# A fused recurrent-attention layer: from steps of 128 tokens of one sequence to steps of 256 tokens of two sequences, with several values kept features-on-partitions

## The reference

```
xn = layernorm(x)
q, k, v = silu(xn @ Wq), silu(xn @ Wk), silu(xn @ Wv)          # [4,512,16,16]
# per head, with decay exp(ld): S_t = exp(ld) S_{t-1} + k_t v_t^T ; o_t = q_t S_t
gate = (xn @ Wg1) @ Wg2                                        # rank 16
o = o * sigmoid(gate); o = o * rsqrt(mean over a head of o*o + 1e-5); o = o * norm_w
s = o @ Wo
g = silu( dequant(fp8(xn * scale)) @ dequant(fp8(W2 * scale1)) )
out = x + s * g
```

## Time and profile before

| | us |
|---|---|
| three runs, median (lowest, highest) | 189.59 (189.05, 189.99) |
| the profiled execution: device time | 189.03 |
| its span, first to last instruction | 187.1 |
| PE busy / DVE busy / POOL busy / ACT busy | 166.7 / 147.3 / 104.6 / 103.1 |
| mean granted TensorE clock, share of full speed | 0.958 |

### The profile page before, as it was taken

One profiled execution on the slowest core, in us unless ns is written; L12 is line 12 of the kernel. 1 busy time (PEld: TensorE's weight loads), 2 busy tenths in 40 slices (PEclk: granted clock), 3 DMA queues, 4 the chain that ended last, 5 costly groups with the idle time before them and its releaser, 6 DMA issues.

```text
span 187.1 us, 7410 instructions
## 1 busy us (share of the span) xinstructions
PE 166.7 (89%) x2510; PEld 127.1 (68%) x2510; DVE 147.3 (79%) x548; ACT 103.1 (55%) x283; POOL 104.6 (56%) x180
## 2 busy tenths in 40 slices
PE   4868469999999999999999999999999999998392
PEld 4745248677777777777777777777777777776181
DVE  1789985979797979888888879797979697857672
ACT  3584446483839383847575665748483847372100
POOL 6654871747565666656574656575747474732210
PEclk9999966999999999999999999999999999999657
DMA  5295300000100010000000000000000000010000
GB/s 145 71 254 166 112 5 0 4 4 4 33 0 32 0 33 4 30 4 28 0 28 0 28 0 27 1 0 28 0 28 0 28 0 28 0 33 4 28 28 28
DMA packets 7201, 5.82 MB, mean 31 GB/s; under 512 B 1744, under 2 KB 7184, under 8 KB 7184
## 3 DMA queue, kind: packets, MB, share of 16 engines
q1 hardware_dynamic: 7184, 5.60, 9.9%
HBM read 3.50 MB, written 2.10 MB: 30 GB/s over the span
## 4 chain that ended last, share of the span: by engine, by line
PE 61%; DVE 12%; ACT 11%; issue 8%; POOL 3%; DMA 3%; SPq 1%; ACTq 0%; DVEq 0%; POOLq 0%
PE b_scores L1081 11%; PE b_xo L1180 8%; PE b_att L1107 5%; PE b_kv L1028 4%; PE b_kv L1033 3%; PE b_kv L1030 3%; PE b_qg L1028 3%; ACT qT L526 3%; PE b_scores L1124 3%; PE b_gate L1067 3%; ACT ffn_silu L509 2%; DVE og L747 2%; ACT e_y L561 2%; PE b_att L1143 2%; PE b_qg L1033 2%
## 5 line engine op out<-in xcount | busy, mean ns | idle before, releaser
L1081 PE MATMUL b_scores<-qT,kT 32*64 32x128 f32 x512 | 31.6, 283 | 1.5 <-DVE probs L717 1.2
L717 DVE TENSOR_TENSOR probs<-b_scores,decay_mask 128x256 f32<-128x256 f32 x64 | 26.6, 418 | 2.6 <-PE b_scores L1081 2.3
L1081 PEld LDWEIGHTS b_scores<-qT,kT 32*64 32x64 f32 x512 | 20.1, 132 | 12.2 <-issue 8.9
L545 ACT ACTIVATE xn<-x_sb,shift,rstd 128x256 f32 (+1 forms) x15 | 9.0, 602 | 35.1 <-DVE shift L681 35.1
L375 POOL TENSOR_TENSOR state_c<-state,own_head 128x256 f32<-128x256 f32 x28 | 20.7, 738 | 11.3 <-DVE state L733 10.2
L345 POOL TENSOR_TENSOR e_sum<-e_y,e_magic 128x256 f32<-128x256 f32 x16 | 11.7, 729 | 25.0 <-DVE e_magic L692 25.0
L384 POOL TENSOR_TENSOR on<-og,og_rs 128x256 f32<-128x256 f32 x15 | 9.3, 622 | 17.3 <-DVE og_rs L776 15.5
L774 DVE SCALAR_TENSOR_TENSOR og_half<-og_y,og_var 128x16 f32<-128x16 f32 x48 | 14.7, 306 | 0.7
L392 POOL TENSOR_TENSOR y<-sg,x_sb 128x256 f32<-128x256 f32 x15 | 11.0, 731 | 6.1 <-DVE sg L787 6.1
L772 DVE TENSOR_TENSOR og_y<-og_rs 128x16 f32<-128x16 f32 x48 | 13.7, 285 | 0.8
L1124 PE MATMUL b_scores<-probs,v_parity 64*32 64x64 f32 x1024 | 14.0, 229 | 0.2 <-DVE probs L717 0.2
(11 more groups left out here) (135 smaller groups left out, 458.7 us busy)
## 6 DMA issues: line engine op xcount, KB each, us to landing
out_dram<-y SPq DMA_DIRECT2D x16, 128.0 KB, 1.7
x_sb<-in_L_attn_x_dram SPq DMA_DIRECT2D x3, 512.0 KB, 3.5
x_sb<-in_L_attn_x_dram SPq DMA_DIRECT2D x1, 384.0 KB, 5.4
w_f<-in_L_attn_Wk_dram SPq DMA_DIRECT2D x1, 256.0 KB, 2.9
w_f<-in_L_attn_Wv_dram SPq DMA_DIRECT2D x1, 256.0 KB, 3.1
w_f<-in_L_attn_Wq_dram SPq DMA_DIRECT2D x1, 256.0 KB, 3.4
w_f<-in_L_ffn_input_dram SPq DMA_DIRECT2D x1, 256.0 KB, 4.1
wo_f<-in_L_attn_Wo_dram SPq DMA_DIRECT2D x1, 256.0 KB, 3.9
```

The source lines that it names most:

```text
L717: v.tensor_tensor(probs[:, r], b_score[r % 2][:, 0:4 * C].rearrange("p (i c) -> p i c", i=4), decay_mask[:, r], ALU.mult).then_inc(s_probs, 1)
L1081: mm = t.matmul(b_score[r % 2][c * C:c * C + C, half * 2 * C:(half + 1) * 2 * C], kT[rows, u, half, c * C:c * C + C], qT[rows, u, half, :, ...
```

## The change

The kernel is written anew. A step now holds 128 tokens of each of two sequences (`S` = 2, `T` = 256 tokens), so there are 8 steps in place of 16; sequence pairs alternate (`pair(n) = n % 2`). The loop is unrolled, with one program line per instruction. These things change in what is done:

- q comes out of its projection with features on partitions (`project_q`), and the Silu for each head parity is taken straight from PSUM, so q is not transposed. The gate's rank-16 values, the gate, the attention output, the FP8 input and the norm stand features-on-partitions too, so the transposes of the gate's stack, of the quantised x and of the output go.
- The state is kept as 32x32 blocks (`state_steps`, `from_state`), and `from_chunk` adds straight into the output in PSUM; `add_chunk` and its copy go.
- The sums over heads are products with a matrix of halves (`head_sums`), and the reciprocal root works on 128x64 in 11 instructions. GpSimd spreads it (`spread_rs`) and TensorE broadcasts it to the features by two float32 products; VectorE then does the head norm.
- The output projection is float32 in one part, in place of three fp32r parts.
- The decayed q goes from VectorE to GpSimd; the last add of the FP8 rounding goes from GpSimd to VectorE.
- All products of `keep_warm` go, as does one Newton-seed instruction.

```diff
-                    t.matmul(dst, xT_hi[:, kk], w_hi[:, kk, a:b], start=(kk == 0), stop=False)
-                for kk in range(KH):
-                    t.matmul(dst, xT_hi[:, kk], w_lo[:, kk, a:b], start=False, stop=False)
-                pe.wait_ge(s_xTlo, num(i, j) + 1)
-                for kk in range(KH):
-                    mm = t.matmul(dst, xT_lo[:, kk], w_hi[:, kk, a:b], start=False, stop=(kk == KH - 1))
-                mm.then_inc(s_done, 1)
...
+            def project_q(n):
+                u = n % 2
+                pe.wait_ge(s_xThi, n + 1)
+                need(pe, s_sg, n - 2)
+                for part in (w_hi, w_lo):
+                    for half in range(KH):
+                        for kk in range(KH):
+                            t.matmul(ps_q[:, half], part[:, 0, kk, half * P:half * P + P], xT_hi[:, u, kk],
+                                     start=(part is w_hi and half == 0 and kk == 0), stop=False, skip_group_check=True)
+                pe.wait_ge(s_xTlo, n + 1)
+                for half in range(KH):
+                    for kk in range(KH):
+                        mm = t.matmul(ps_q[:, half], w_hi[:, 0, kk, half * P:half * P + P], xT_lo[:, u, kk],
+                                      start=False, stop=(kk == KH - 1), skip_group_check=True)
+                for s in range(S):
+                    tok = slice(s * P, s * P + P)
+                    for kk in range(KH):
+                        t.matmul(dst[:, s], xT_hi[:, u, kk, tok], w_hi[:, w, kk], start=(s == 0 and kk == 0), stop=False, skip_group_check=True)
+                        t.matmul(dst[:, s], xT_hi[:, u, kk, tok], w_lo[:, w, kk], start=False, stop=False, skip_group_check=True)
+                    for kk in range(KH):
+                        mm = t.matmul(dst[:, s], xT_lo[:, u, kk, tok], w_hi[:, w, kk], start=False, stop=(kk == KH - 1), skip_group_check=True)
...
-                    t.transpose(ps_qT[:, kk, :], q[:, kk * P:kk * P + P], ident[:])
-                        mm = t.matmul(ps_state[b * C:b * C + C, half, :], kd[rows, u, cols],
-                                      kv[rows, u, D + cols.start:D + cols.stop], start=True, stop=True)
-                                mm = t.matmul(ps_avT[32 * r:32 * r + 32, half, c, :],
-                                              v_parity[rows, u, par * D + half * P + 32 * r:par * D + half * P + 32 * r + 32],
-                        t.matmul(ps_o[c * C:c * C + C, half * P:half * P + P], qdT[:, u, half, c * C:c * C + C],
-                                 st[:, half, :], start=(half == 0), stop=False, skip_group_check=True)
-                        mm = t.matmul(ps_o[:, half * P:half * P + P], avT[:, half, :], ident[:],
-                                      start=False, stop=True, skip_group_check=True)
-                    mm = t.transpose(ps_oT[:, kk, :], on[:, kk * P:kk * P + P], ident[:])
-                parts = [(oT_hi, wo_hi), (oT_hi, wo_lo), (oT_lo, wo_hi)]
-                for n, (lhs, rhs) in enumerate(parts):
-                    for kk in range(KH):
-                        mm = t.matmul(ps_out, lhs[:, kk], rhs[:, kk], start=(n == 0 and kk == 0), stop=(n == 2 and kk == KH - 1))
...
+                for half in range(KH):
+                    mm = t.matmul(ps_gate[:, half], wg2_stack[:, half * P:half * P + P], g1T[:], start=(half == 0), stop=True, skip_group_check=True)
+                else:
+                    pe.wait_ge(s_probs, 4 * n + r - 1)
+                            mm = t.matmul(ps_score[r % 2][c * C:c * C + C, cols], kT[rows, u, half, tok],
+                                          q_par[rows, u, :, half, tok], start=True, stop=True, skip_group_check=True)
+                mm.then_inc(s_score, 1)
+                                mm = t.matmul(ps_u[32 * r:32 * r + 32, c, half, s], kd[rows, u, s, half * P + 32 * r:half * P + 32 * r + 32],
+                                              heads[:, s * HH + half * 4 + r, :, 0:E], start=True, stop=True, skip_group_check=True)
+                mm.then_inc(s_u, 1)
+                pe.wait_ge(s_qd, n + 1)
+                pe.wait_ge(s_ownmid, n + 1)
+                if pos(n) < NB - 1:
+                    pe.wait_ge(s_end, ends(n))
+                if pos(n) > 0:
+                    pe.wait_ge(s_ownend, ends(n - PAIRS))
+                                t.matmul(ps_o[rows, c, z:z + C], st, qd[rows, u, half, s * P + c * C:s * P + c * C + C],
+                                         start=(half == 0 and s == 0), stop=False, skip_group_check=True)
+                                    mm = t.matmul(ps_o[32 * r:32 * r + 32, c, z:z + C], v_par[rows, u, blk:blk + 2 * E],
+                                                  probs[rows, r, s, i:i + C],
+                                                  start=(c == 0 and pos(n) == 0 and half == 0 and s == 0 and par == 0),
+                                                  stop=(par == 1), skip_group_check=True)
+                mm.then_inc(s_ops, 1)
+            def head_sums(n):
+                pe.wait_ge(s_sq, n + 1)
+                            mm = t.matmul(ps_sum[32 * j:32 * j + 32], head_sum[:, half, 0:32], og_sq[:, c, z:z + C],
+                                          start=(half == 0), stop=(half == KH - 1), skip_group_check=True)
+            def spread_rs(n):
+                pe.wait_ge(s_spread, n + 1)
+                if known(n + 2):
+                    pe.wait_ge(s_xTlo, n + 3)
+                for half in range(KH):
+                    mm = t.matmul(ps_rs[:, half], head_spread[:, half], rs_spread[:].rearrange("p j t -> p (j t)"),
+                                  start=(half == 0), stop=True, skip_group_check=True)
+                mm.then_inc(s_rsps, 1)
+            def project_o(n):
+                pe.wait_ge(s_on, n + 1)
+                if known(n + 2):
+                        mm = t.matmul(ps_out[:, s], on[:, kk, s * P:s * P + P], wo_scaled[:, kk], start=(s == 0 and kk == 0),
+                                      stop=(kk == KH - 1), skip_group_check=True)
+                mm.then_inc(s_outps, 1)
...
+                nxt, cur, back = known(n + 1), known(n), known(n - 1)
+                if n == -1:
+                    pe.wait_ge(s_wlo, 1)
+                if cur:
+                    scores(n, 0)
+                    scores(n, 1)
+                if nxt:
+                if cur:
+                    scores(n, 2)
+                    scores(n, 3)
+                if nxt:
+                    project_k(n + 1)
+                if cur:
+                    state_steps(n)
+                if nxt:
+                    project_g1(n + 1)
+                if back:
+                    spread_rs(n - 1)
+                if nxt:
+                    project_v(n + 1)
+                    if n == -1:
+                    if n == -1:
+                    ffn(n + 1)
+                if cur:
+                    from_state(n)
+                    from_chunk(n)
+                if known(n + 2):
+                    transpose_x(n + 2)
+                if nxt:
+                    transpose_k(n + 1)
+                if back:
+                    project_o(n - 1)
+                if cur:
+                    head_sums(n)
...
+                g.tensor_tensor(e4_sum[:], e4_y[:], e4_magic[:], ALU.add).then_inc(s_e4sum, 1)
+                pool.wait_ge(s_e4sum, n + 1)
+                need(pool, s_xqT, n)
+                g.tensor_tensor(e4_q[:], e4_sum[:], e4_magic[:], ALU.subtract).then_inc(s_e4q, 1)
+                g.tensor_tensor(rs_spread[:], og_rs[:].unsqueeze(1).broadcast_to([P, 4, C]),
+                                own_block[:].unsqueeze(2).broadcast_to([P, 4, C]), ALU.mult).then_inc(s_spread, 1)
+                g.tensor_tensor(y[:, n % 2], sg[:].rearrange("p (s d) -> p s d", s=S), x_sb[:, x_tiles(n), :], ALU.add).then_inc(s_y, 1)
...
+                nxt, cur, back = known(n + 1), known(n), known(n - 1)
+                if nxt:
+                    round_y(n + 1)
+                if nxt:
+                    decay_q(n + 1)
+                if back:
+                    spread_rs(n - 1)
+                if nxt:
+                    decay_k(n + 1)
+                if cur:
+                    own_state_mid(n)
+                    own_state_end(n)
+                if known(n - 2):
+                    add_x(n - 2)
+                if known(n + 3):
+                    norm_factors(n + 3)
...
+                if known(n + 2):
+                    high_xT(n + 2)
+                    scale_y(n + 2)
+                if nxt:
+                    copy_kT(n + 1)
+                if cur:
+                    square_o(n)
...
+                v.tensor_tensor(probs[:, r], ps_score[r % 2].rearrange("p (s z) -> p s z", s=S),
+                                decay_mask[:, r].unsqueeze(1).broadcast_to([P, S, 4 * C]), ALU.mult).then_inc(s_probs, 1)
+                v.scalar_tensor_tensor(out=og[:], in0=gate_tanh[:, n % 2], scalar=1.0, in1=ps_o,
```

(45 more changed lines are left out.)

1499 lines of the change are left out of this document (614 added, 885 removed).

## The result

The changed kernel takes 199.09 us (median of 4 runs, 197.87 to 202.58), the kernel before 189.42 beside it: ratio 1.0487, 95% interval 1.0427 to 1.0546, slower by 4.9%. The forecast was 187.0. The profiled execution took 197.87, its span (first to last instruction) 196.1, against 184.5 forecast for the span: 11.6 us to find.

The account below looks back on a forecast made before the run. TensorE was taken to bound the kernel: 15.3 us of work plus 3.5 of waits per cycle, 18.8 with switches. With both ends the span came to 184.5, plus 1.9 outside and 0.56 for the median: 187.0 us, range 171 to 196.

Parts of the forecast that it names:

- F0: End of step 0's from_chunk products, which frees TensorE (F in any cycle): forecast at 44.7 us.
- undisturbed period, 18.8: TensorE's cycle for 256 tokens: 15.3 us of work and 3.5 of waits, 18.8 with half of the rounded-away switches.
- hindrance of VectorE by GpSimd: VectorE instructions with two SBUF inputs, and find_nan, wait out GpSimd's: TensorE waits 1.4 us at mask 0, 1.0 before FFN.
- slower rival: GpSimd's decayed q stops VectorE's root once more, delaying mask 0: period 20.0, 194 us in all; 24%.
- step 1 17.3: Step 1, without output add and with half of the state products, was to take 17.3 us.
- handover to the head sums: After the output projection TensorE waits for ScalarE's square before the head sums: stall 0.35 us.
- this rival: TensorE's clock stays low over many cycles; dismissed as having little for it, with no chance of its own.
- From the chunk: 1.55: TensorE's products from the chunk: 32 took 0.79 us, so 64 of the same shape take 1.55 per cycle.
- the number of records is what is equal: Reason for costing the 32 smaller state products at 0.8 us, between bounds of 0.38 and 0.79.
- the 15.3 of the sum: TensorE's work in a new cycle, all products added: 15.3 us against 19.44 before.

Follow-up runs that it names:

- a_addx: Changed kernel with GpSimd's add of the output moved from behind the masked end state to behind spread_rs: 197.63 us, or 195.41 without disturbed runs.
- a_warm: Changed kernel plus 56 idle identity products (before the first FFN, first scores, first head sums, and in the drain): 194.46 us, ratio 1.0296.
- a_combo_inter: Changed kernel with idle products, moved output add, masks 0 and 1 before the whole root, and two score groups taken product by product: 184.16 us, ratio 0.9746.
- a_combo: Changed kernel with 56 idle products, moved output add, and masks 0 and 1 ahead of the whole reciprocal root: 185.36 us, ratio 0.9734.
- ci_split: a_combo_inter with the row of 128 chunk products cut in half by the transposes of x and k: 183.62 us, ratio 0.9711.
- b_twice_loop: Kernel before, loop kept, with each chunk's products of probabilities and values computed twice: 219.67 us, or 217.8 without disturbed runs.
- a_split: Changed kernel with the row of 128 chunk products cut in half by the transposes of x and k: 205.81 us, ratio 1.0878.

## Why the prediction was wrong

**Right.** The rows of single parts: F0 at 44.98 (44.7 forecast), the first scores at 32.08 (31.2), the row of 128 records 1.41 to 1.49 (1.55), the state products 0.69 (0.8, with bounds of 0.38 and 0.79), the output projection 1.89 (1.8), the broadcast 1.03 (0.9), the next scores 3.29 behind F (3.4). The undisturbed period, 18.8, to the tenth, twice. And the hindrance of VectorE by GpSimd, the cause of both waits in the cycle (0.92 each, where 1.4 and 1.0 were forecast):

```profile
113.32 1.29 POOL L324 TENSOR_TENSOR e_q<-e_sum,e_magic 128x512 bf16<-128x512 f32 x1
113.33 1.36 DVE L647 TENSOR_TENSOR og_y<-og_rs 128x64 f32<-128x64 f32 x1
...
122.32 1.29 POOL L363 TENSOR_TENSOR y<-sg,x_sb 128x512 f32<-128x512 f32 x1
122.40 1.36 DVE L585 TENSOR_SCALAR e_nan<-e_q 128x512 bf16<-128x512 bf16 x1
```

og_y takes 1.36 us under GpSimd's rounding, 0.23 alone, and find_nan 1.36 under the output's add, 0.29 alone (a_addx). The hindrance of the slower rival, by the decayed q, came too (og_y at 116.32, 0.71 us), behind mask 0 and so at no price: the slower rival's mechanism did not decide. The Trainium skill (SBUF — State Buffer, "Who interferes with whom") holds here as it did in the prediction: VectorE waits out the whole instruction that was first.

**Wrong, two terms that stood at nothing.**
1. *Step 1's clock.* The step that failed is "step 1 17.3", with the low clock put only on step 0's first 3 us and on the end of the drain. I had costed the handover to the head sums at 0.35, from a steady cycle. In step 0 there is no output projection beside it, so TensorE idles 1.93 us at 47.99, after a step 0 that itself had holes, and the clock is 0.50 from 50 to 62 us. Price in us: 22.9 - 17.3 - 0.9 for the stop in it = 4.7; a_warm, with its products there, does the step in the 17.3 of the forecast. I had let this rival go with "the waits are 1.5 and 1.0 us in a cycle", without looking at the one step that differs.
2. *Stops without a wait.* "From the chunk: 1.55" took 0.79 for 64 records and doubled it. The time of a record was right (128 in 1.41), but in four of the rows TensorE also stops for 0.9 to 1.5 us, and once behind one: 0.89 + 0.94 + 1.41 + 0.93 + 1.52 = 5.7. A row of 64 in the kernel before shows no such stop in 16, nor in 16 written out; rows of 128 do, in that kernel too. The kernel before could not show it, but the same step had written "the number of records is what is equal" and never asked how many records a microsecond TensorE can be given over a longer stretch; the new cycle has 192 in 2.5 us, where the old had 64 amid wide ones.

Together 10.4 of the 11.6 us. The other 1.2 are the drain, 27.9 us against 26.7, and that is the clock again: the last step's states and chunk, forecast to end 9.5 us behind its first scores, end 10.75 behind them (168.18 to 178.93), and what follows takes 17.2 as forecast. The forecast had the low clock from the broadcast on only.

```profile
172.00:178.00 6.00, 6.00 (x210) 4.62 (x211) 2.62 (x7) 0.00 (x0) 2.24 (x3) 0.50 0.15 49
```

That the sum closes to the tenth is in part luck: against the forecast, F0 is 0.3 late, steps 2 and 3 are 0.6 longer than their stops explain and step 6 is 1.0 shorter.

A smaller term was wrong too and hidden: a pair of score groups takes 1.52, not 1.05, because groups written one behind the other overlap less than I read from 4 products in a group to 8 in two; a_combo_inter shows 1.03 with the right order. In the changed kernel the first pair's excess lies in the wait for mask 0 (0.92 waited where 1.45 was forecast), and for the second the forecast had masks as the bound anyhow, 1.65 for both groups. So the work of a cycle is not the 15.3 of the sum: with both waits gone, a_combo still takes 16.9, and TensorE is busy for 16.5 of 16.8 us in it (63.7 to 80.5).

That the stops are the fetching of instructions is the reading that fits all of it: fixed places in the program whatever the times, evenly spaced in its records, a shift by inserted instructions, none at 64 records, many at 128, and the same 1.2 to 1.6 us from the end of a packet to TensorE's next product. Fewer stops when wide products part the same instructions fit too, but weakly (ci_split). What stays open is how early a packet is asked for, and why the third turn of the loop in b_twice_loop has to fetch where the kernel before does not.

## What to carry to other kernels

Count instructions, not only columns: many small products in an unbroken row can run out of fetched instructions. A written-out program doesn't bring this on by itself, and a loop is no sure protection: of three turns one ran without packets and stops. A cycle's price from steady rows doesn't hold for the first cycle and the last; look for the one idle time there that a neighbour's work used to fill, since it can cost the clock of a whole step. And judge a single edit in an undisturbed cycle as well as by the time of the run: each of the two waits was worth 1.1 us a cycle, while the clock and the stops elsewhere ate part of it. With the idle products in, both waits gone, and the order of the scores and the FFN's place changed, the same design takes 180.5 us, 4.4% under the kernel before.

## What the runs showed of the hardware

- Small products (64 rows by 32 columns out, 64 columns in) go at 11 to 12 ns a record, and a row of 128 stopped 0.2 to 2.0 us at places fixed in the program; the same instructions with 1 us of wide products in the middle stopped 0.4 to 0.6 in a_split, at a mean clock of 0.84, and 0.5 to 1.7 in ci_split, at 0.96.
- 53 of 54 stops of more than 0.3 us ended 1.16 to 1.58 us behind the end of a 16 KB packet of the instruction queue.
- b_twice_loop has 11.6 us of stops in all, its written-out form 7.6; in the second turn of the loop no packet came (88 to 131 us) and no row stopped.
- After 1.9 us of idleness the clock was at 0.50 for 12 us in which TensorE was busy throughout (50 to 62). In a_split it fell in four cycles behind a wait of 1.54 to 1.56; in the changed kernel waits of 0.92 at the same place cost no clock, in a_addx it was at 0.50 behind one of them (117 to 119.5).
- Two row groups of scores take 1.52 us one behind the other and 1.03 product by product.
